# Five weight remainders move from VectorE to GpSimd, and the first convolution's SiLU and split move ahead of weight part 3

## The reference, cut to what matters

```python
x = x + _layernorm(_L0_attn_ref(_layernorm(x), ...))
x = x + _layernorm(_L0_ffn_ref(_layernorm(x), ...))

def _L0_attn_ref(x, ...):
    x = _lin(x, w1)
    x = _depthwise_conv(x, conv_w, conv_b)
    x = jax.nn.silu(x)
    x_delta = jax.nn.softplus(_lin(x, dl_w, dl_b))
    A_t = _lin(x, A_w, A_b)
    A_bar = jnp.exp(-x_delta * A_t)
    B_x = _lin(x, B_w, B_b)
    A_cum = jnp.cumprod(A_bar, axis=1)
    h = jnp.cumsum(B_x * A_cum, axis=1)
    ssm_out = _lin(h, C_w, C_b) + _lin(x, D_w, D_b)
    x_res = jax.nn.silu(_lin(ssm_out, w2))
    return ssm_out + _lin(ssm_out * x_res, w3)
```

## Time and profile before

| | |
|---|---|
| median of 3 runs | 1121.13 us (1115.91 to 1122.24) |
| profiled execution | 1116.39 us, of which the span 1114.5 us |
| PE / PEld | 1022.9 / 902.9 us busy (92% / 81%) |
| DVE / ACT / POOL | 801.9 / 623.8 / 286.8 us busy (72% / 56% / 26%) |
| chain that ended last | PE 75%, DVE 11%, DMA 4%, issue 3%, POOL 3%, ACT 2% |
| mean granted TensorE clock | 0.978 of full |

### The profile page before, as it was taken

The page is one execution under the profiler, slowest core; times in us unless marked ns, Lnnn a source line. Parts: engine busy times, 40 slices in busy tenths (PEclk is TensorE's granted clock), DMA queues, the critical chain, the costliest instruction groups (busy, mean ns, idle before and its releaser), DMA issues.

```text
span 1114.5 us, 21512 instructions
## 1 busy us (share of the span) xinstructions
PE 1022.9 (92%) x7026; PEld 902.9 (81%) x7026; DVE 801.9 (72%) x2059; ACT 623.8 (56%) x1265; POOL 286.8 (26%) x303
## 2 busy tenths in 40 slices
PE   4889999989998999899999999999999999999930
PEld 2666677667676566799999999999999999999930
DVE  4997799888888857766666666666666666666645
ACT  6867868786876446344454444444544445445425
POOL 1133123453262273212121121211211212122134
PEclk9899999999999999999999999999999999999975
DMA  8656667886576588955563521735366822655149
GB/s 302 219 198 207 221 222 228 272 263 219 165 263 213 182 274 305 379 198 174 151 218 74 216 36 21 266 107 178 66 229 225 288 35 36 213 181 159 25 120 200
DMA packets 116518, 210.30 MB, mean 189 GB/s; under 512 B 9952, under 2 KB 75232, under 8 KB 116448
## 3 DMA queue, kind: packets, MB, share of 16 engines
q1 hardware_dynamic: 101040, 189.51, 49.0%
q0 software_dynamic: 15408, 19.93, 10.5%
HBM read 341.43 MB, written 86.02 MB: 384 GB/s over the span
## 4 chain that ended last, share of the span: by engine, by line
PE 75%; DVE 11%; DMA 4%; issue 3%; POOL 3%; ACT 2%; SPq 0%; DVEq 0%; ACTq 0%; POOLq 0%
PE bank L488 12%; PE bank L1461 10%; PE bank L1463 10%; PE bank L1462 10%; PE bank L1506 5%; PE bank L1508 5%; PE bank L1507 5%; PE bank L482 4%; PE bank L483 3%; PE bank L484 3%; POOL xs_scratch L1232 2%; DMA w_both<-w_split 1%; DVE h L925 1%; PE bank L1447 1%; PE bank L1479 1%
## 5 line engine op out<-in xcount | busy, mean ns | idle before, releaser
L1409 POOL DMA_INDIRECT acc_scratch<-cv,ids x71 | 111.5, 1571 | 504.1 <-DVE cv L1606 494.4
L1643 DVE TENSOR_SCALAR cv<-bank 128x256 f32<-128x256 f32 x284 | 120.5, 424 | 155.1 <-PE bank L1463 136.3
L1573 ACT ACTIVATE cv<-cv 128x256 f32<-128x256 f32 x284 | 118.4, 417 | 183.7 <-DVE cv L1643 183.7
L1461 PE MATMUL bank<-h_hi,w_both 128*128 128x256 f32 x640 | 178.0, 278 | 2.2 <-DMA w_both<-w_split 1.0
L1463 PE MATMUL bank<-h_hi,w_both 128*128 128x256 f32 x640 | 177.2, 277 | 0.0
L1462 PE MATMUL bank<-h_hi,w_both 128*128 128x256 f32 x640 | 177.2, 277 | 0.0
L1559 ACT ACTIVATE h_lo<-cv 128x256 fp32r<-128x256 f32 x256 | 106.8, 417 | 92.1 <-DVE cv L1646 92.1
L1646 DVE TENSOR_TENSOR cv<-bank,cv 128x256 f32<-128x256 f32 x284 | 120.3, 424 | 41.7 <-ACT cv L1573 34.6
L1461 PEld LDWEIGHTS bank<-h_hi,w_both 128*128 128x128 f32 x640 | 120.2, 188 | 3.1 <-issue 2.3
L1463 PEld LDWEIGHTS bank<-h_hi,w_both 128*128 128x128 f32 x640 | 120.3, 188 | 0.0
L1462 PEld LDWEIGHTS bank<-h_hi,w_both 128*128 128x128 f32 x640 | 120.3, 188 | 0.0
(11 more groups left out here) (293 smaller groups left out, 2819.1 us busy)
## 6 DMA issues: line engine op xcount, KB each, us to landing
w_both<-w_split SPq DMA_DIRECT2D x155, 776.0 KB
single_ring<-w_split SPq DMA_DIRECT2D x14, 3880.0 KB
w_split<-e_both SPq DMA_DIRECT2D x128, 256.0 KB, 4.0
e_both<-w_e SPq DMA_DIRECT2D x64, 384.0 KB, 3.5
h_lo<-w_split SPq DMA_DIRECT2D x31, 776.0 KB
xs_lo<-w_split SPq DMA_DIRECT2D x31, 776.0 KB
single_ring<-w_split SPq DMA_DIRECT2D x14, 1552.0 KB
w_split<-e_both SPq DMA_DIRECT2D x64, 264.0 KB, 3.7
```

Of the source, the lines that this page charges most:

```text
L1461: nc.tensor.matmul(out, gu_hi[f][:, cols], xg_hi[:, par, c, :], start=c == 0, stop=False)
L1643: nc.vector.tensor_scalar(half, gate_ps, CLIP, -CLIP, ALU.min, ALU.max).then_inc(clipped, 1)
```

## The change

`split_low` leaves VectorE's program and stands in GpSimd's, with the same wait and the same arithmetic, directly behind the two inverse roots of sequence 0. On ACT, `p3/0 w2/0` move from ahead of `S0/0` to behind `r1/0`; on DVE `w2/0` moves from ahead of `r0/0` to behind `r1/0`. The rest of the table is only broken into other lines.

```diff
 "scalar":
-... c0/0 c1/0 p3/0 w2/0 S0/0 S1/0 r0/0 r1/0 c2/0 c3/0 w3/0 p4/0 S2/0 be0/0 S3/0 ...
+... c0/0 c1/0 S0/0 S1/0 r0/0 r1/0 p3/0 w2/0 c2/0 c3/0 w3/0 p4/0 S2/0 be0/0 S3/0 ...
 "vector":
-m0/0 m1/0 k/0 p0/0 p1/0 w0/0 p2/0 w1/0 c0/0 c1/0 p3/0 w2/0 r0/0 r1/0 c2/0 c3/0 m0/1 w3/0 dt0/0 p4/0 da0/0 ...
+m0/0 m1/0 k/0 w0/0 w1/0 c0/0 c1/0 r0/0 r1/0 w2/0 c2/0 c3/0 m0/1 w3/0 dt0/0 da0/0 ...
 "gpsimd":
-m0/0 m1/0 m0/1 lo0/0 ...
+m0/0 m1/0 p0/0 p1/0 p2/0 p3/0 p4/0 m0/1 lo0/0 ...
...
-            def split_low(b, n):
-                at, src, chunks = weights[n]
-                cols = slice(at, at + chunks * src.shape[1])
-                dve.wait_ge(w_hi_ready, n + 1)
-                nc.vector.tensor_tensor(w_lo[:, cols], raw_w[:, cols], w_hi[:, cols], ALU.subtract).then_inc(w_lo_ready, 1)
...
+            def split_low(b, n):
+                at, src, chunks = weights[n]
+                cols = slice(at, at + chunks * src.shape[1])
+                pool.wait_ge(w_hi_ready, n + 1)
+                nc.gpsimd.tensor_tensor(w_lo[:, cols], raw_w[:, cols], w_hi[:, cols], ALU.subtract).then_inc(w_lo_ready, 1)
...
-            run("gpsimd", {"m": x_root, "tab": make_tables, "lo": h_remainder, "d": d_stage})
+            run("gpsimd", {"m": x_root, "p": split_low, "tab": make_tables, "lo": h_remainder, "d": d_stage})
```

More of the change, by code:

```diff
@@ L1077, in fullest @@
                 i.then_inc(star_ready, 1)
-            run("vector", {"x": first_lo, "star": fullest, "m": x_moments, "p": split_low, "k": bias_sum, "c": conv_sides, "r": xs_remainder, "dt": delta_unit, "da": da_unit,
+            run("vector", {"x": first_lo, "star": fullest, "m": x_moments, "k": bias_sum, "c": conv_sides, "r": xs_remainder, "dt": delta_unit, "da": da_unit,
                            "ac": acum_unit, "bx": bx_unit, "h": h_unit, "d": d_stage, "w": w_stage,
```

## The result

The changed kernel takes 1123.37 us (median of 20 runs, 1120.67 to 1126.62); the kernel before, run beside it on the same chip, takes 1118.77 us (20 runs, 1115.91 to 1122.24). The ratio is 1.0036, 95% interval [1.0026, 1.0045]. That is 4.0 us slower (2.9 to 5.0), a real loss and under the 0.5% bound. The forecast was 1123.3 us, with a range of 1117 to 1129.

What follows compares the result with a forecast made beforehand. PE bounds the kernel from 70 us on; before that, when ACT reaches S3 decides. +3.2 us less 0.6 for the clock gave +2.6, 1123.7 on the 1121.1 median, put at 1123.3; range 1117 to 1129.

Steps and rivals of the forecast that it cites:

- p0 leaves DVE: GpSimd's shift nm no longer slowed by p0, so ACT's wait at 11.65 goes: -0.73 us, bounds 0 and -0.73.
- p1 and p2 for nothing: On GpSimd at about 15.7 to 20.7 us, while DVE has only expert chunks 0 and 1: cost 0.
- ACT's order uses up the gain: p3 and w2 ahead of c2 and c3 on ACT: 1.7 us against PE's 1.6 gained, S3 +0.1 us.
- Part 3 blocks chunk 2: GpSimd's p3, 2.5 us from 30.2, holds DVE's w2 until 32.7; S3 at 36.6, running sum +1.9 us.
- Part 4 gets in between the taps: GpSimd's p4 runs 1.3 us between c2's side taps on DVE; S3 at 37.9, running sum +3.2 us.
- p4's removal gains nothing at dt0: p4 (0.68 us) leaves DVE behind dt0, but dt1 waits for ACT's ln1: gain 0.
- Expert chunks hidden: w2 and w3 come 2 to 3 us later on DVE; ACT's idle stretch of 3.55 us covers it.
- An earlier clock in the first product: PE's pause ahead of its second transposes disappears, so its clock may rise sooner: -0.6 us, bounds 0 and -1.2.
- rival B: PE idles 4.8 us ahead of dl2 and its clock falls again, adding 2.2 us: 1127; chance 0.15.
- Rival A: No block of DVE by GpSimd, or an earlier clock: +0.1, with full clock gain -1.1 us, 1120.0; chance 0.15.
- C: DVE catches up between dt0 and 68 us, +1.9 turns to about +1; chance 0.12 with D and anything unseen.
- D: GpSimd's weight parts late for PE's dl0, b0 or d0.0; no size; chance 0.12 with C and anything unseen.

Runs made afterwards that it cites:

- order-only kernel: Against before: all five remainders stay on DVE, first SiLUs and splits of x come ahead of part 3 and chunk 2; ratio 1.0035 [1.0014, 1.0056].
- these three parts alone: Against before: only weight parts 0 to 2 moved to GpSimd, every other order kept; ratio 0.9994 [0.9972, 1.0016].
- third experiment: Against after: GpSimd's parts 3 and 4 put behind the inverse root of sequence 1, at 37 us; ratio to before 1.0017 [0.9993, 1.0041].
- in pieces: Against after: GpSimd's parts 3 and 4 cut into instructions of 256 columns; ratio to before 0.9999 [0.9972, 1.0027].
- sixth experiment: Against after: 14 products whose result nobody reads added on PE between A1 and dl2; ratio to before 1.0005 [0.9982, 1.0028].
- PE kept warm: Against weights early: 24 products that nobody reads added on PE between u3 and dl0; ratio to before 0.9998 [0.9983, 1.0012].
- weights early: After with only part 0 on GpSimd, parts 1 to 4 on DVE during the first product, chunk 2 ahead of x's split; ratios to before 0.9992 and 0.9988.

## Why the prediction was right, and where it wasn't

1. *p0 leaves DVE.* Forecast: `nm` at 0.20, ACT's 0.73 us of idling gone. Right: `nm` took 0.20 at 10.46. The first product started at 14.80 instead of 15.75, of which 0.15 us is that DVE's moments began earlier (7.76 instead of 7.91). The order-only kernel, which keeps p0 on DVE, has `nm` at 0.92 and 0.65 us of idling on ACT. The front as a whole scatters as much as this step is worth: even in the order-only kernel c1's taps ended 0.81 us earlier than in before.
2. *p1 and p2 for nothing.* Right: they ran from 15.60 to 20.27 while DVE had little to do, and the kernel with these three parts alone keeps 6.33. Where part 2 held an expert chunk, DVE's idling took it up.
3. *dl0 at 29.5.* It came at 29.30.
4. *ACT's order uses up the gain.* Right. The forecast's net +0.1 holds -0.73 for the front, so +0.84 for the order, all of it on ACT's queue; the third experiment measured +0.98, of which 0.82 are ACT's queue and 0.16 a wait for DVE's last tap. What the forecast did not count is that DVE now idles 1.22 us ahead of the split of x. With part 3 on GpSimd this costs at most the 0.16; with part 3 still on DVE the same order costs 1.38 (the second experiment).
5. *Part 3 blocks chunk 2.* Forecast 2.5 us for GpSimd's 128x1024, measured 2.39; chunk about 2.7, measured 2.52; a cost of +1.8 (steps 4 and 5), measured +1.57 by the chunk's length.
6. *Part 4 gets in between the taps.* Forecast +1.3, measured +0.92. S3 was forecast at 36.6 to 37.9 and came at 37.02. The third experiment removes both blocks by moving the GpSimd instructions, so their cause is shown. The opening's sentence that the engines hold each other back only by semaphores is therefore too strong: here GpSimd held DVE with no semaphore between the two instructions.
7. *p4's removal gains nothing at dt0.* Right: dt0 was 2.36 us later, as S3 was.
8. *Expert chunks hidden.* Right, as far as the chain shows: no wait for a load stands in it before 48 us.
9. *An earlier clock in the first product, -0.6.* In the profile after it was worth 0.14: 8.11 us against 8.25. A single trace can't settle it, as the next profile of the same kernel had 0.87 less. Over all traces, in the view that gives 8.44 and 8.30 for these two, the three that keep the wait for `nm` took 7.99 to 8.76 us (mean 8.40) and the nine without it 7.03 to 8.30 (mean 7.65), so a gain of about the forecast's size is likely. That the clock was the cause is inferred: single matmuls there took 1.06 us and 0.59 us, while the profile's column of the granted clock reads 1.00 for the whole product.

The failed part is the weight given to rival B: the sum has no term for the clock behind PE's pause ahead of dl2. B's mechanism, that PE's longer wait for dt0 costs it its clock at dl2, happened in both profiles of after and in the kernel in pieces, and the sixth experiment takes it away by filling the pause. The prediction gave it 0.15 and measured it by the 4.6 us for which PE had stood still in before; pauses of 3.90, 3.49 (in pieces) and once even 2.02 us were followed by a low clock. Its price was forecast at 2.2 us and was 0.88 at bx0 (2.05 in the second profile). In before DVE already waited 0.59 us for PE ahead of bx0, and in after 1.47, which is the same 0.88; where the rest of the price went was not tested. A further 0.6 at 68 us was in no case of the prediction. It came in six of the ten experiments too: the seven traces with a low clock between 62 and 72 us need 28.96 to 29.03 from bx0 to s0, and the five without need 28.42 or 28.43. With both, the delay at `s0` is 2.36 + 0.88 + 0.60 = 3.84 us, against 4.0 [2.9, 5.0] measured over the whole kernel; that the first number makes the second is plausible and not shown, since single executions differ by more than that behind 72 us.

The prediction's last sentence said that the forecast as a whole fails if PE's clock is low after 40 us. By that sign it failed: the clock was 0.50 from 41 to 44. The account of how the 4 us come about was incomplete, and that the number fits is luck in part.

So the forecast of 1123.3 hit for two reasons. The mechanism that it put first was right, and its sum of +2.6 came out as +2.36 at S3: the front gave 1.09 us where 0.73 and 0.6 were counted, the order cost 0.98 for 0.84, the chunk 1.57 for 1.8 and the tap 0.92 for 1.3. And two misses offset each other: the base, the median of 1121.1 from three runs, lay 2.4 us above the one of 1118.8 from twenty (these three among them), while 1.5 us of clock were left out and 0.4 us taken off at the end for the spread of the runs. Rival A (no block) is out by after's own rows and by the third experiment, C because the delay of S3 was all there at `s0`, D because every weight part was ready in time (part 0 at 12.98, part 2 at 20.27, part 4 at 34.99).

What stays open: the second ratio for the same kernel, 1.0010 [0.9989, 1.0032], overlaps the first only between 1.0026 and 1.0032, so the loss is best put at about 3 to 4 us, and it may be smaller. The order-only kernel lost 1.6 to 6.3 us where its trace at `s0` shows 1.1. What makes the stretch between 72 and 474 us of one kernel last 13 us longer in one execution than in another was not settled; four low clock stretches and three long waits for an unknown queue lie in it, but no run isolated them.

The Trainium skill, "SBUF — State Buffer", section "Who interferes with whom", names the lock and what escapes it. The runs here agree in both: a subtraction, a scan and the convolution's taps, with two SBUF inputs, were held (2.52, 1.64, 1.67 us), and `dt`, `da` and the moments, with one, kept their length beside the same instructions (`dt` 0.75 at 38.35 and `da` 0.74 at 39.90 in the kernel with parts 3 and 4 late, the moments 1.39 in the kernel in pieces).

## What to carry to other kernels

Free time on GpSimd is only free while VectorE isn't reading two inputs from SBUF. Before an element-wise instruction with SBUF inputs goes to GpSimd, list what DVE runs in its whole duration; a long GpSimd instruction beside a chain of short DVE ones can get in at a semaphore between two of them, and costs the chain up to its full length. Put it where DVE idles, or works from PSUM, and cut it only if the pieces cost less than the block.

When work is moved out of a gap, look at what the gap is left with. Here part 3 was filling 1.2 us in which DVE waits for ACT anyway, so taking it off the chain gained nothing on the next link; putting another piece that was due into the same gap was the only version that came out faster, and only just. And if a delay lengthens a pause of TensorE, count the low clock behind it as a term of the sum, at the rows' half rate for as long as another engine is waiting for it.

## What the hardware did that was not expected

- The low clock came after short pauses of PE too: 0.51 from 38 to 41 us after a pause of 2.02 us. Yet in the kernel with PE kept warm, pauses of 2.06 us ahead of dl0 and of 1.88 us ahead of dl2 had none behind them.
- The same work can be followed by it or not: the two pauses between bx0 and s0 are 1.19 to 1.20 and 2.16 to 2.20 us in before, after, order only, weights early, in pieces, PE kept busy and kept warm, and the clock fell near the end of the second in all of these but before.
- The same kernel (before) showed no low stretch between 42 and 1060 us in one execution and four in another. Where a low stretch could be priced in these traces it cost 0.53 to 0.61 us (between bx0 and s0) or 0.84 to 2.05 us (between dt0 and bx0, in after and in pieces).
- GpSimd's subtraction took 2.36 to 2.39 us for 128x1024, 1.30 for 128x512, and 6.84 for six of 128x256 with DVE's instructions between them: about 1.14 for each.
- A GpSimd instruction that had to wait shows the wait inside its own duration (1.62 instead of 1.30), and so does DVE's (2.52 instead of 0.95). Neither appears as idle time in brackets.
